# GpSimd takes more rows of blocks 1 and 2, the last block ends by chunks, and all orders are redrawn

## What is computed

```python
# attention: 16 heads of 8 features
q, k, v = x @ Wq, x @ Wk, x @ Wv
fg = sigmoid(x @ Wf + bf)
def step(state, inp):                       # state: batch, head, i, j
    state = state * gt[..., None] + vt[..., None] * kt[..., None, :]
    out_t = einsum('bhij,bhj->bhi', state, qt)
out = layernorm(out) * gamma + beta
x = layernorm(x + (out * silu(x @ Wg)) @ Wout)
# network, 512 wide; every weight is ternary times a scale per output
h = silu(lin(x, w1)) * lin(x, w2)
h = gelu(lin(h, h1)); h = gelu(lin(h, h2))
x = layernorm(x + lin(h, w3))
```

## Time and profile before

| | us |
|---|---|
| median of three runs | 512.54 |
| the profiled execution | 511.54 |
| its span, first to last instruction | 509.6 |
| TensorE busy | 496.3 (97%) |
| VectorE busy | 448.7 (88%) |
| ScalarE busy | 406.4 (80%) |
| GpSimd busy | 311.7 (61%) |

### The profile page before, as it was taken

How to read it: one execution, slowest core, us unless ns; L and a number is a source line. 1 busy time by engine, 2 the same in 40 slices (tenths; PEclk the granted TensorE clock), 3 DMA queues, 4 the chain that set the end, 5 groups by cost and what they waited for, 6 DMA issues and landing times.

```text
span 509.6 us, 7946 instructions
## 1 busy us (share of the span) xinstructions
PE 496.3 (97%) x2528; PEld 382.4 (75%) x2528; DVE 448.7 (88%) x708; ACT 406.4 (80%) x839; POOL 311.7 (61%) x363
## 2 busy tenths in 40 slices
PE   8999999999999999999999999999999999999995
PEld 5576777777878777786877777786877777787995
DVE  4999989999999899998999999899999999993352
ACT  5775968888887888978797788988778987868863
POOL 0751848668392766848385765938477683929432
PEclk9999999999999999999999999999999999999998
DMA  6899999953994497689969675799719483710001
GB/s 244 205 267 236 255 263 241 230 125 84 275 221 104 104 246 177 154 195 249 259 183 234 142 185 125 186 222 244 196 51 235 130 194 94 183 25 1 23 23 44
DMA packets 21500, 87.33 MB, mean 171 GB/s; under 512 B 2512, under 2 KB 3280, under 8 KB 13520
## 3 DMA queue, kind: packets, MB, share of 16 engines
q1 hardware_dynamic: 21168, 86.46, 67.9%
q10 hardware_dynamic: 288, 0.33, 0.2%
HBM read 74.72 MB, written 12.06 MB: 170 GB/s over the span
## 4 chain that ended last, share of the span: by engine, by line
PE 48%; POOL 17%; DVE 13%; issue 13%; ACT 7%; DMA 1%; POOLq 0%; DVEq 0%; ACTq 0%
PE F L2342 26%; POOL h1lo L479 5%; PE front L2243 5%; POOL h2lo L479 5%; PE back L2441 4%; DVE KJ L1590 3%; DVE QJ L1597 2%; POOL KJ L541 2%; DVE QJ L1605 2%; PE ps_v L2243 2%; PE back L2328 2%; PE back L2227 1%; DMA out<-res 1%; POOL rstd_o L511 1%; POOL y L553 1%
## 5 line engine op out<-in xcount | busy, mean ns | idle before, releaser
L903 ACT ACTIVATE h<-F,cols 128x512 f32<-128x512 f32 x120 | 80.7, 686 | 17.0 <-PE F L2342 16.5
L479 POOL TENSOR_TENSOR h1lo<-h,h1hi 128x512 fp32r<-128x512 f32 x60 | 76.5, 1291 | 12.8 <-ACT h1hi L896 12.7
L547 POOL TENSOR_TENSOR QJ<-QJ 128x512 f32<-128x512 f32 x14 | 18.0, 1284 | 108.0 <-DVE QJ L1605 108.0
L479 POOL TENSOR_TENSOR h2lo<-h,h2hi 128x512 fp32r<-128x512 f32 x60 | 77.2, 1309 | 4.9 <-ACT h2hi L896 4.7
L1590 DVE TENSOR_TENSOR_SCAN KJ<-g,carry,KJ 128x512 f32<-128x512 f32 x64 | 78.5, 1263 | 0.9 <-ACT carry L829 0.8
L1590 DVE TENSOR_TENSOR_SCAN KJ<-g,KJ 128x512 f32<-128x512 f32 x64 | 74.3, 1202 | 1.6 <-POOL KJ L528 0.7
L1597 DVE TENSOR_TENSOR QJ<-QJ,KJ 128x1024 f32<-128x1024 f32 x60 | 72.9, 1237 | 0.2
L2342 PE MATMUL F<-h2hi,whi 128*128 128x512 f32 (+1 forms) x256 | 71.6, 415 | 0.8 <-ACT h L903 0.7
L2342 PE MATMUL F<-h1hi,whi 128*128 128x512 f32 (+1 forms) x256 | 68.9, 410 | 1.6 <-DVE h L1654 1.3
L2342 PE MATMUL F<-h1lo,whi 128*128 128x512 f32 (+1 forms) x256 | 67.4, 400 | 0.2 <-POOL h1lo L479 0.2
L2342 PE MATMUL F<-h2lo,whi 128*128 128x512 f32 (+1 forms) x256 | 65.7, 397 | 0.0
(11 more groups left out here) (184 smaller groups left out, 935.9 us busy)
## 6 DMA issues: line engine op xcount, KB each, us to landing
KJ<-qk_bounce SPq DMA_DIRECT2D x30, 1024.0 KB, 9.9
QJ<-qk_bounce SPq DMA_DIRECT2D x30, 1024.0 KB, 11.0
qk_bounce<-qk SPq DMA_DIRECT2D x30, 256.0 KB, 4.6
x_in<-in_x SPq DMA_DIRECT2D x16, 256.0 KB, 11.4
xT<-in_xT SPq DMA_DIRECT2D x15, 256.0 KB, 11.5
out<-res SPq DMA_DIRECT2D x15, 256.0 KB, 3.3
wraw<-in_wffn SPq DMA_DIRECT2D x2, 1024.0 KB, 6.6
wraw<-in_wffn SPq DMA_DIRECT2D x2, 256.0 KB, 4.6
```

The lines of the kernel that those rows point to most:

```text
L479: e.tensor_tensor(h_lo[layer][:, t, :w], h[:, t, :w], h_hi[layer][:, t, :w].bitcast(f32), ALU.subtract).then_inc(lo_done[layer], 1)
L547: e.tensor_tensor(first, first, other, ALU.add).then_inc(add_gp_done, 1)
L903: e.activation(dst[:, t, :WIDTH[n]], F[t][:, :WIDTH[n]], ACT.Gelu, scale=scale[t]).then_inc(gelu_done[layer], 1)
```

## The change

- In block 1 POOL makes all eight products of K rows and v (four before) and the products of Q rows and state for j = 0 to 3 (none before, new function `qs_gp`); in block 2 it makes four of the former (two before). DVE makes the others, two rows in an instruction. The tables `KV_FIRST` and `QS_FIRST` hold the split, and the semaphore counts follow from them.
- The last block's end goes by chunks of 128 tokens. The product by w3 of a chunk (`last_block`) signals for itself; `residual_last` adds x1; `square_last` makes the mean square in one DVE instruction with a summed output, over 129 columns, the last of which holds the square root of 128 times epsilon; `rstd_last` is one power on POOL; `scale_last` (ACT) and `scale_end` (DVE) scale. Three stores of 2, 1 and 1 chunks take the place of two. No mean is subtracted here: w3 is centered already, as for the other blocks.
- `save_carry(15)`, which nobody read, is left out. The network of block 0 waits for two split weight pieces at its start and for the others at its middle layers.
- The five orders and the table `FREED` are new in many places.

```diff
+    KV_FIRST, QS_FIRST = {1: 0, 2: 2}, {1: 2}
...
+            def qs_gp(n, j):
+                if j % 2 == 0:
+                    e.wait_ge(Q_landed[2 * j // HD][n % 2], fetched(n))
+                e.wait_ge(scan_done, HD * n + j + 1)
+                Q = rows(QJ, n)[:, j, :]
+                e.tensor_tensor(Q, Q, rows(KJ, n)[:, j, :], ALU.mult).then_inc(qs_gp_done, 1)
...
+            def rstd_last(c):
...
+                cs = slice(0, 2) if c == 1 else slice(c, c + 1)
+                e.wait_ge(squared_last, c + 1)
+                e.tensor_tensor(rstd["2"][:, (NB - 1) % 2, cs], square2[:, cs], mhalf4[:, cs], ALU.pow).then_inc(pow_last_done, 1)
...
+            def residual_last(c):
+                e.wait_ge(w3_last_made, c + 1)
+                e.wait_ge(oT_made, NB - 1)
+                e.tensor_tensor(last_res[:, c, :D], F[c][:, chunk(c)], x1[(NB - 1) % 2][:, chunk(c)], ALU.add).then_inc(r2_last_done, 1)
...
+            def square_last(c):
...
+                e.scalar_tensor_tensor(last_sq[:, c, :D + 1], last_res[:, c, :D + 1], 1.0 / D, last_res[:, c, :D + 1],
+                                       ALU.mult, ALU.mult, accum_out=square2[:, c:c + 1]).then_inc(squared_last, 1)
...
+            def last_block(c):
+                h_ = c // NL
+                for k in range(NH):
+                    e.wait_ge(gelu_half_done[2][h_], k + 1)
+                    last = e.matmul(F[c][:, chunk(c)], h[:, k, chunk(c)], w3[:, k, :], start=k == 0, stop=k == NH - 1)
+                last.then_inc(w3_last_made, 1)
```

More of the change, by code:

```diff
@@ L200, in half_bank @@
             return (F, (ps_v, g, front, back))[half][t]
+        assert NB % 2 == 0 and NC_ == 2 * NL
+        last_res, last_sq = (QJ[NB % 2][:, a * NC_ * 2 * D:(a + 1) * NC_ * 2 * D].rearrange("p (c d) -> p c d", c=NC_) for a in range(2))
         def half_up(half, t, which):
@@ L1937, in _ @@
             hmul(6, 0)
+            residual_2(5)
+            hmul(6, 1)
             kv(8, 0)
-            hmul(6, 1)
-            residual_2(5)
             hmul(6, 2)
```

1386 lines of the change are left out of this document (693 added, 693 removed).

## The result

The changed kernel is slower: 514.85 us median of 22 runs (512.62 to 515.85) against 512.48 us of 22 runs of the kernel before (511.17 to 513.15), a ratio of 1.0049 with a 95% interval of 1.0041 to 1.0056. I had forecast 510.0 and given "slower" 0.16. The profiled execution took 515.29 around a span of 513.4 (before: 511.54 around 509.6).

What follows compares the result with a forecast made beforehand. TensorE, busy 97% of the span, was taken as the bound. Head -1.4, end -1.1 and middle 0 sum to -2.5 us: profiled 511.54 becomes 509.0, the median 510.0 us; range 507.8 to 513.6.

Steps and rivals of the forecast that it cites:

- item 1: Head: ScalarE's early sum of low parts makes the first scan 0.7 us later and block 0's statistics 0.5 us late.
- item 2: Head: GpSimd makes five v products of block 1 before block 0's deviation, so its power comes at 29.5, not 29.05.
- item 3: Head: fewer VectorE scans and state products ahead of block 0's x1 low part; first silu 2.4 us early.
- Item 4: Head: block 3's projection q no longer fills TensorE's wait, so block 0's middle products start only 1.4 us early.
- Rival A: Head: VectorE and GpSimd exclude each other over SBUF; two meetings eat the 1.4 us, giving 511.4; chance 0.16.
- Rival B: Head: block 1's Q rows are issued at 31.3 and land late; 512.6 to 515.4 us; chance 0.10.
- The middle: Blocks between head and end: no product added or removed, so 0 us, bounds -2 and +3.
- Rival C: Middle: projections stand at other places and 10 us of waits become 13; 513.0 us; chance 0.09.
- gate projection "taken as nothing": Block 14: the gate projection moves to block 13; at most 0.9 us lost, taken as nothing.
- The end: After the last product: chain by chunks of 1.7 us against 3.15, less 0.4 lost at the gelu; net -1.1 us.
- the PE tail: Last block: TensorE's last product ends 26.7 us after its first 256-column product, 0.4 more than before.

Runs made afterwards that it cites:

- x5_wait_filler: The changed kernel with GpSimd waiting for VectorE's x1 scalings in block 0 and 8 instead of 16 filler products before x1's transposes; 512.77 us.
- h6_filler: The kernel before with the new end, block 14 normalised and stored early, and 8 instead of 16 filler products before block 0's x1 transposes; 510.43 us.
- x3_gate: The changed kernel with block 15's gate projection back behind block 14's last w1/w2 products; 515.23 us.
- h1_end: The kernel before with only the new end, block 14's normalisation as late as in the changed kernel; 512.63 us.

## Why the prediction was wrong

- **First scan and statistics of block 0 (item 1): right.** 11.38 and 27.97 for 11.1 and 27.7; in the mean of the profiles the first scan is 0.5 us later than in the old orders, 0.7 forecast. I took two things as fixed that are not: the landing that the new order waits for differs by up to 1.8 us between executions (ACT's first sum at 6.87 to 8.72), and the old orders' first scan by 1.1, by the pace of PE's first products. The 10.37 that I started from was an early one.
- **Deviation of block 0 (item 2): right in kind, small in size.** Power at 30.07 for 29.5.
- **The gain of the head (item 3): the step that failed.** Gated product 34.07 (33.5), deviation 39.5 (38.9) stood. "Normalises from 39.3; transposes at 40.2" did not. The two scalings of x1 took 2.50 us for 0.6, and I had not counted the 17 filler products that the new PE list has behind the count of the low parts, although the same list gave me all other steps there. With either one left, the gain did not come: 0.94 us back without the collision, 0.03 with the shorter filler, 1.90 with both. The rest of the step is right: with both gone (x5_wait_filler) x1's low part is at 42.21 and block 1 at 73.39, and h6_filler confirms that DVE's state products were what held it before. The term was -1.4. Measured, it is +1.35 between the two profiles, or about +0.9 with the first scan at its mean (0.5, and 0.34 from there to block 1). Once both limits are gone, the head is 1.6 us shorter than the old one from the first scan on (62.43 to 63.98), about 1.0 with item 1's loss taken off.
- **Item 4: right.** From the first silu to the 32 transposes of block 1 it is 4.8 us (46.01 to 50.83), 4.5 forecast and 3.5 before.
- **Rival A (the port): the right mechanism at a place that I did not look at.** I looked for products with two SBUF inputs and wrote "the gated product" and "the first state product of block 2" (that one did take 1.95 us, at 60.41). The scaling has one tensor input and seemed safe. The section of the Trainium skill that I had cited ("SBUF — State Buffer", "Who interferes with whom") also says that `tensor_scalar` from and to SBUF can take both ports and then shuts GpSimd out, or waits for it. The trace agrees, 1.27 and 1.31 us for 0.32 and 0.34, and 0.39 with the input in PSUM. At 1.9 us in one place it costs more than the 0.6 to 1.0 that I gave a meeting, because an instruction of 0.3 us waits for one of 1.27.
- **Rival B (late Q rows): false.** Issued at 31.79 (I said 31.3); POOL's first state product starts at 39.66 without a wait.
- **The middle: 0, with bounds -2 and +3.** It cost 1.86 between the two profiles, 1.7 in the mean. Rival C, to which I gave 0.09, held for the middle. The gate projection "taken as nothing" is right (x3_gate). That all projections stand earlier is what I passed over; whether that is the cause stays open.
- **The end: the chain right, the store wrong, the second step that failed.** 1.62 us for 1.7; the PE tail 26.49 for 26.7. The term was -1.1 and measured +0.6, as from the last scaling to the end of the span it took 4.04 us for 2.2. The saved 1.5 us went because I let the store take what it took before. I did not ask what else is on the DMA engines at the new time: block 14's 256 KB, issued at 508.08, and PE's instruction fetch.
- **The chances.** 0.66 for faster rested on two gains in which something was left out each time: PE's queue and DVE against POOL in the head, the other packets on the DMA engines at the end.

## What to carry to other kernels

When work moves to GpSimd, list every VectorE instruction in that window that reads and writes SBUF, the short scalings and copies too, and price each at the length of the GpSimd instruction that it can meet. When a gain is argued along one engine's list, read the lists of all engines up to the same point, filler included: a step is as early as the latest of them, and with two limits at one place one edit alone shows a part of the gain or nothing. Before a landmark is compared between two profiles, compare an earlier one too: here 1.01 of the head's 1.35 us were there at the first scan, half of that by the spread of the start. At the end of a kernel the last transfer competes with the one before it and with instruction fetches; put large stores well ahead of it, and try the end alone before tying it to other edits.

## What the runs showed of the hardware

- A `tensor_scalar` of 128x128 fp32 from SBUF to SBUF on VectorE takes 0.32 to 0.35 us alone and 1.27 to 1.31 us beside GpSimd instructions of 1.27 us; from PSUM it takes 0.39 beside the same.
- PE's instruction fetches are single packets of 16 KB on one of the 16 DMA engines, 0.9 to 1.6 us long. Two come at the end of its program, 3.1 to 3.8 us apart. A last store of 64 KB whose packets on that engine are behind one lands 3.0 to 3.8 us after its issue instead of 1.5 to 1.7.
- The first weights' landing moves by over 1 us between executions of the same code (7.47 and 8.72 for ACT's first sum). So does the pace of PE's first products: the first two projections of the kernel take 1.88 us in the profile of the kernel before and 2.77 us in h1_end, with the same code up to there.
